# The output product of each expert block, written as three fp32r products with split operands

## The reference

```python
logits = xt @ router_w + router_b
scores = softmax(logits) + router_bias      # two groups of four, then the two best experts
def step(y, p):
    w1, b1, w2, b2, w3, b3, ge = p
    h = silu(xt @ w1 + b1) * (xt @ w2 + b2)
    return (y + ge[:, None] * (h @ w3 + b3), None)
y, _ = scan(step, zeros_like(xt), (ew1, eb1, ew2, eb2, ew3, eb3, gate.T))
z = silu(xt @ sw1 + sb1) * (xt @ sw2 + sb2) @ sw3 + sb3   # shared expert
x = x + y + z
```

## Time and profile before

| what | value |
|---|---|
| median of 3 runs | 371.08 us (370.57 to 374.64) |
| the profiled execution's own time | 369.3 us |
| its span | 367.5 us |
| TensorE busy | 337.1 us, 92% of the span |
| VectorE busy | 184.3 us, 50% |
| ScalarE busy | 117.5 us, 32% |
| GpSimd busy | 102.7 us, 28% |
| `bh` products, line 1503 | 62.4 us, 496 records |
| output products, line 1476 | 31.6 us, 62 records |

### The profile page before, as it was taken

The page is one execution under the profiler, slowest core; times in us unless marked ns, Lnnn a source line. Parts: engine busy times, 40 slices in busy tenths (PEclk is TensorE's granted clock), DMA queues, the critical chain, the costliest instruction groups (busy, mean ns, idle before and its releaser), DMA issues.

```text
span 367.5 us, 5442 instructions
## 1 busy us (share of the span) xinstructions
PE 337.1 (92%) x1923; PEld 248.0 (67%) x1923; DVE 184.3 (50%) x366; ACT 117.5 (32%) x203; POOL 102.7 (28%) x131
## 2 busy tenths in 40 slices
PE   8878898999999989999896599899998999999993
PEld 3356687459888778887765334458887877888872
DVE  2636893446848613364258617935420346542267
ACT  0655301013373214363102653572221334222110
POOL 2050000423666776774230000199600000000000
PEclk9998999559999999999999579999999999999997
DMA  6899910155767676999969986000000000110003
GB/s 209 278 340 404 383 45 0 29 192 193 220 194 238 208 243 186 320 361 395 398 248 339 333 307 223 0 3 0 0 2 0 0 3 0 64 52 0 1 2 114
DMA packets 32313, 59.94 MB, mean 163 GB/s; under 512 B 6680, under 2 KB 7548, under 8 KB 32286
## 3 DMA queue, kind: packets, MB, share of 16 engines
q1 hardware_dynamic: 25182, 48.89, 38.2%
q0 software_dynamic: 5056, 8.49, 6.9%
q10 hardware_dynamic: 2048, 2.21, 1.8%
HBM read 55.02 MB, written 12.40 MB: 183 GB/s over the span
## 4 chain that ended last, share of the span: by engine, by line
PE 69%; DVE 11%; DMA 7%; issue 7%; ACT 3%; POOL 3%; ACTq 0%; POOLq 0%; DVEq 0%; SPq 0%
PE bank L1503 13%; PE bank L408 10%; PE bank L410 10%; PE bank L409 10%; PE bank L1476 5%; PE bank L1487 4%; PE bank L1470 3%; PE bank L1569 3%; DMA xrow<-xstage 2%; DMA yg<-ytok 2%; PE bank L1325 2%; DMA xg<-xrow,tokx 1%; DVE acc L1200 1%; DVE upl L1220 1%; PE bank L1407 1%
## 5 line engine op out<-in xcount | busy, mean ns | idle before, releaser
L1503 PE MATMUL bank<-xt,ew 128*128 128x128 f32 x496 | 62.4, 280 | 2.0 <-issue 2.0
L1503 PEld LDWEIGHTS bank<-xt,ew 128*128 128x128 f32 x496 | 59.3, 196 | 4.3 <-issue 4.1
L595 POOL DMA_INDIRECT xg<-xrow,tokx x31 | 33.1, 1067 | 56.3 <-DVE dstx L1025 33.1
L602 POOL DMA_INDIRECT ytok<-yout,dstx x31 | 31.8, 1027 | 30.7 <-DVE yout L1136 21.5
L1284 DVE TENSOR_TENSOR sq<-rel 128x512 f32<-128x512 f32 x16 | 13.4, 837 | 43.3 <-ACT rel L846 43.3
L756 ACT ACTIVATE xt<-bank 128x512 f32<-128x512 f32 x31 | 18.5, 597 | 41.4 <-PE bank L1470 41.3
L1476 PE MATMUL bank<-ew,bhid 128*128 128x512 f32 x62 | 31.6, 595 | 0.0
L1470 PEld LDWEIGHTS bank<-ident,xg 128*128 128x128 f32 x124 | 15.8, 146 | 18.3 <-issue 14.2
L408 PE MATMUL bank<-dnh,sqh 128*128 128x512 f32 x64 | 25.2, 393 | 1.8 <-DVE sql L1292 1.6
L408 PE MATMUL bank<-ah,uph 128*128 128x512 f32 x64 | 25.1, 392 | 0.0
L410 PE MATMUL bank<-dnh,sql 128*128 128x512 f32 x64 | 24.9, 389 | 0.0
(11 more groups left out here) (299 smaller groups left out, 612.0 us busy)
## 6 DMA issues: line engine op xcount, KB each, us to landing
ew<-in_L_ffn_ew SPq DMA_DIRECT2D x51, 256.0 KB, 3.7
ew<-in_L_ffn_ew SPq DMA_DIRECT2D x21, 512.0 KB, 7.8
toep<-kpad SPq DMA_DIRECT2D x4, 1536.0 KB, 11.6
yg<-ytok SPq DMA_DIRECT2D x8, 512.0 KB, 4.6
acc<-in_x SPq DMA_DIRECT2D x4, 512.0 KB, 7.3
xrow<-xstage ACTq DMA_DIRECT2D x4, 512.0 KB, 7.5
upraw<-in_L_ffn_up_w SPq DMA_DIRECT2D x1, 2048.0 KB, 10.4
dnraw<-in_L_ffn_down_w SPq DMA_DIRECT2D x1, 2048.0 KB, 13.3
```

The source lines that it names most:

```text
L595: pool.indirect_dma_start(xg[:, n % XGS, :], None, xrow, bass.IndirectOffsetOnAxis(ap=tokx[:, n:n + 1].bitcast(U32), axis=0), bounds_check ...
L602: pool.indirect_dma_start(ytok, bass.IndirectOffsetOnAxis(ap=dstx[:, n:n + 1].bitcast(U32), axis=0), yout[:, n % YOS, :], None, bounds_che ...
L1503: mm = pe.matmul(bank[2 + n % 2][:, w * P:(w + 1) * P], ew[:, ring(n), col + k * P:col + (k + 1) * P], xt[:, n % 2, k, :], start=(k == 0), ...
```

## The change

Line numbers in this section are those of the kernel before. The output product of block n becomes three fp32r products by `split3`. Per block, ACT writes the rounded `w3h` from the block's `w3` in the ring (128 x 512) and the rounded `bhh` from `bhid` (128 x 128). DVE writes the remainder of `w3` in place into the ring (`ewl`, the same memory as `ew`, 128 x 512) and the remainder of `bhid` (`bhl`, 128 x 128). `w3h` has two buffers over the memory of `silu`, `bhh` and `bhl` have three each. Every block's copies and remainders stand at fixed places of the two lists.

```diff
     silu = at(exp_reg, "silu", [P, 2, HALF])
...
+    r = [silu_at]
+    w3h = at(r, "w3h", [P, 2, T], F32R)
+    r = [toep_at]
+    ewl = at(r, "ewl", [P, RING, WCOLS], F32R)
...
+    bhl = at([early[0] - BHS * P * 4], "bhl", [P, BHS, P], F32R)
...
+    bhh = at(small, "bhh", [P, BHS, P], F32R)
...
             act.activation(bsil[:, n % 2, :], bank[2 + n % 2][:, 0:P], ACT.Silu, bias=b1).then_inc(bsil_ok, 1)
+            act.wait_ge(*weights_in(n))
+            wait(act, by_done, n - 1)
+            act.activation(w3h[:, n % 2, :], ew[:, ring(n), W3], ACT.Copy).then_inc(w3h_ok, 1)
             if n + 2 < NB:
                 x_copy(n + 2)
+            act.wait_ge(bhid_ok, n + 1)
+            act.activation(bhh[:, n % BHS, :], bhid[:, n % BHS, :], ACT.Copy).then_inc(bhh_ok, 1)
...
             if n >= 2:
                 y_copy(n - 2)
+            dve.wait_ge(w3h_ok, n + 1)
+            tt(ewl[:, ring(n), W3], ew[:, ring(n), W3], f(w3h[:, n % 2, :]), ALU.subtract).then_inc(w3l_ok, 1)
+            dve.wait_ge(bhh_ok, n + 1)
+            tt(bhl[:, n % BHS, :], bhid[:, n % BHS, :], f(bhh[:, n % BHS, :]), ALU.subtract).then_inc(bhl_ok, 1)
...
         def block_y(n):
-            pe.wait_ge(bhid_ok, n + 1)
+            pe.wait_ge(bhl_ok, n + 1)
+            pe.wait_ge(w3l_ok, n + 1)
             wait(pe, yout_ok, n - 1)
-            pe.matmul(bank[6 + n % 2][:, :], bhid[:, n % BHS, :], ew[:, ring(n), W3], start=True, stop=True)\
-                .then_inc(by_done, 1)
+            split3(pe, bank[6 + n % 2][:, :], lambda k: (bhh[:, n % BHS, :], bhl[:, n % BHS, :]),
+                   lambda k: (w3h[:, n % 2, :], ewl[:, ring(n), W3]), 1).then_inc(by_done, 1)
```

More of the change, by code:

```diff
@@ L132, in adaln_ffn_program @@
     sw3raw = at(exp_reg, "sw3raw", [P, SH * T])
+    silu_at = exp_reg[0]
     silu = at(exp_reg, "silu", [P, 2, HALF])
@@ L345, in adaln_ffn_program @@
     warm_ok = sem("warm_ok")
+    w3h_ok, w3l_ok, bhh_ok, bhl_ok = (sem(s) for s in ("w3h_ok", "w3l_ok", "bhh_ok", "bhl_ok"))
     b3_done, b3_added = sem("b3_done"), sem("b3_added")
```

## The result

The changed kernel takes 379.32 us, the median of four runs (378.82 to 379.84); the kernel before took 370.98 in four runs beside them. The ratio is 1.0203, with a 95% interval of 1.0137 to 1.0268. It is slower by 8.3 us. I had forecast 374.2 us in a range of 370 to 378.5: the sign is right, the size is not, and the time lies above the range. The profiled execution took 379.51 us, its span is 377.8 (369.3 and 367.5 before).

What follows compares the result with a forecast made beforehand. TensorE (92% busy) was taken to bound only blocks to 8 and 15 to 21, POOL 8 to 17, the DMA queue from 21. 3.4 + 0.4 - 0.9 + 0.2 = +3.1 us on 371.08 gave 374.2 us, range 370 to 378.5.

Steps and rivals of the forecast that it cites:

- what one block costs: Expert stage, TensorE: three fp32r products take 0.68 us instead of 0.86, so a block takes 2.91 us instead of 3.09.
- the lag of DVE in blocks 2 to 5 and ACT's place in it, +3.4: DVE falls behind in blocks 2 to 5, ACT's sines and exponential wait, and POOL's chain from block 6 starts 3.4 us later.
- DVE's own two operations take 1.01 (96.01 to 97.02): DVE's existing work per block, 1.01 us, counted with 0.88 of remainders and 2.3 of convolution steps as 4.2 us a block.
- One addition ... I add 0.4 (0 to 2): POOL, blocks 8 to 17: remainders with two SBUF inputs slow some seven indirect DMAs and the small operations, +0.4 us.
- the second rival: DVE and POOL slow each other from block 8 on; POOL sets the pace, 4.8 us more, 379 us; chance 0.17, slower.
- the 383 us of the prediction: Time if every POOL gather and scatter pair lost both remainders, 0.88 us, in every block, by the skill's rule taken literally.
- the weights of block 28 land as much later as their queue began: Blocks 21 to 30: bytes and rate unchanged, so these weights shift with their queue and TensorE's faster pace becomes waiting.
- -0.9: Blocks 17 to 21: five blocks give back 0.18 us each before the first Toeplitz tile is let go, -0.9 us.
- the clock: Rival: TensorE's clock falls in the waits before blocks 8 and 10; two blocks cost 6 us, 380 us; chance 0.06.
- the tail: After block 30: the last output product waits for its new operations, mostly hidden by a 1.20 us scatter wait; +0.2 us.

Runs made afterwards that it cites:

- early splits only: Three fp32r products with their copies and remainders in blocks 0 to 13 only, later blocks as in the kernel before; 376.16 us, 1.0116 against the kernel before.
- late splits: Three fp32r products with their copies and remainders in blocks 14 to 30 only, earlier blocks as in the kernel before; 372.63 us, 1.0032 against the kernel before.
- splits from block 8: Three fp32r products with their copies and remainders from block 8 on, blocks 0 to 7 as in the kernel before; 374.57 us, 1.0096 against the kernel before.
- products only: Changed kernel with three products per block of operands rounded in blocks 0 and 1, other copies and all remainders dropped; 372.55 us, 1.0022 against the kernel before.
- operations only: Changed kernel keeping all four new operations per block, but with one float32 product of the two remainders; 376.06 us, 1.0110 against the kernel before.
- useless matmuls: Changed kernel plus filler matmuls into an unused bank: four before block 15's transposes, five before block 28's input products; 376.96 us, 1.0123 against the kernel before.

## Why the prediction was right in sign and wrong in size

**Right: what one block costs, and what ACT and DVE pay.** I had a block at 2.91 us; it is 2.93. The three products take 0.78 from the first to the next operation, not 0.68; half of the saving came from the place ahead of them, which I hadn't counted, and made up for it. From `w3h` to the next operation it is 0.52, from `bhh` 0.22, from `ewl` 0.60, from `bhl` 0.20 (differences of starts in the same timelines), against 0.53, 0.22, 0.61 and 0.27.

**Right in mechanism, 0.8 too large: the lag of DVE in blocks 2 to 5 and ACT's place in it, +3.4.** DVE has no idle time from block 2 to the `bhid` of block 6 but 0.44 us at two fills with zeros, and that `bhid` starts at 108.38 (forecast 106.5, with a start of the stage that is 2.8 us later in this profile). From there to `bsil` of block 8 it is 7.2 us, forecast 7.1. The scatter of block 6 is 2.6 us later, not 3.4: mis-sized by 0.8. The size was lost in "DVE's own two operations take 1.01 (96.01 to 97.02)": in this stretch of 1.01 us DVE idled for some 0.15, and where DVE doesn't idle the two take 0.86 (104.23 to 105.09). With 0.20 for `bhl`, not 0.27, the four blocks took 15.8 us (`bhid` of block 2 at 92.61, of block 6 at 108.38) and not 16.8. The waits of TensorE before blocks 8 and 10 came out at 0.99 and 1.86 (forecast 1 to 2 and 2); that before block 7 did not come.

**Wrong: "One addition ... I add 0.4 (0 to 2)".** This term measured +2.2, and 2.3 with the lag taken away. I had looked at the indirect DMAs, and their mean grew only from 1.05 to 1.12 us. The price fell on the 15 small operations that I had named in the same sentence and not priced: one of 0.22 us takes up to 0.76 beside a DVE operation with two SBUF inputs. The rule in the second rival, that "only an operation that starts under one is lengthened", held, but 15 short operations in a row start under many. The rival "DVE and POOL get in each other's way throughout" had the mechanism and the wrong place: it is not throughout, since the lateness was 4.8 us at gather 15 and 3.6 at block 27.
The Trainium skill (SBUF — State Buffer, "Who interferes with whom") says that a DVE instruction with two SBUF inputs contends with a GpSimd instruction that reads SBUF, and one with at most one doesn't. The small operations agree: 0.76 beside `ewl`, 0.22 at the same place when the remainder's input comes from PSUM. That the loser is blocked for the whole instruction agrees with them too: the one at 122.58 ends 0.09 us behind the `ewl` of 122.57 to 123.25. For the DMAs that GpSimd issues the same section of the Trainium skill infers that a `tensor_tensor` doesn't hold them up, so the 383 us of the prediction stretched the rule beyond that section. The trace lies between: single scatters that started under such operations took 1.42 to 1.78 us instead of 1.0, while the mean of all 62 grew by 0.07.

**Wrong: "the weights of block 28 land as much later as their queue began", with "the bytes to be moved and the rate are as before", and -0.9 kept.** The rate is as before, the bytes are not. From the issue of the first Toeplitz pair to the products of block 28 it took 20.2 us before (155.71 to 175.89) and 22.7 after (162.93 to 185.62). The DMA view of exactly that stretch, before and then after (queue, packets, MB, share of the 16 engines; q1 is SP's, q0 POOL's gathers and scatters):

```profile
DMA packets 3630, 7.61 MB, mean 377 GB/s; under 512 B 490, under 2 KB 490, under 8 KB 3627
...
q1 hardware_dynamic: 2733, 5.27, 71.8%
q0 software_dynamic: 894, 2.31, 30.9%
```

```profile
DMA packets 4125, 8.74 MB, mean 385 GB/s; under 512 B 556, under 2 KB 556, under 8 KB 4123
...
q1 hardware_dynamic: 3077, 5.90, 71.1%
q0 software_dynamic: 1046, 2.81, 32.3%
```

1.13 MB more, at 385 GB/s, is 2.9 us. With the rate nearly the same a longer stretch must hold more bytes, so this count says what was moved and not yet why. POOL's part of it is 0.50 MB or 1.3 us, and it goes with TensorE's pace: q0 moves 2.31 MB in this stretch before and 2.34 with early splits only, where the late blocks have the float32 product, and 2.77, 2.79 and 2.79 with late splits, splits from block 8 and products only, where they have three (operations only, at the old pace, lies between with 2.55). The stretch of the kernel with splits from block 8 is nearly as long as before (20.5 us), so there it isn't the length that makes the bytes. In the timelines one more gather falls into the stretch: that of block 26 starts 0.29 us behind the issue of the first pair, where it was 0.73 ahead of it, and the last scatter starts 18.30 us behind it, not 19.25. That these bytes hold up the weights is not shown: with splits from block 8 they are all there, and block 28 comes only 0.3 us later behind the issue. The other part, 0.63 MB of SP's (SyncE's) own queue, follows no such rule: it is 5.27 before, 5.90 in the changed kernel, 5.34 with early splits, 5.57 with late ones and 5.03 with splits from block 8. Whether it is a backlog from before the stretch or the second pair of tiles, which was issued 5.1 us ahead of block 28 here and 1.7 before, stays open. So block 28 is 4.4 us later because its queue began later (the mechanism forecast, with 2.9), and 2.5 more behind that; those 2.5 are the failed step, and only part of them, if any, goes with POOL's bytes. The 1.75 us that TensorE had won since block 16 (forecast 0.9) only made its wait longer.

**Wrong: the clock, put at nothing in the sum and at 0.06 as a rival.** The waits before blocks 8 and 10 (0.99 and 1.86 us) cost no clock in this profile of the changed kernel; that was luck, for in two others with the same early blocks (early splits, useless matmuls) the input products of block 10 took 3.04 and 3.28 us behind the same wait. It fell in the two longer waits, for which I had foreseen no price at all, since the wait of 1.35 us before block 28 had cost nothing. The input products behind them took 1.7 and 1.5 us more, together half of the rival's 6 us. With the fillers block 30 comes 2.4 to 3.1 us earlier.

**Right in size, by another way: the tail.** I had +0.2 (0 to 0.6), in the shade of a scatter. From block 30 to the first convolution product it is 29.6 us before and after. But the chain of waits of the changed kernel no longer goes through that scatter; it goes through the wait of the last product for `bhl` (1.01 us) and the products behind it:

```profile
196.52 0.30 DVE bhl L1164
...
196.86 0.50 PE bank L416
...
206.63 0.75 DVE acc L1217
```

So this wait now lies on the path, though the way through it is no longer than the old one was.

In short, the steps that failed: the "one addition" of 0.4, which measured 2.2; the way to block 28, which was to give back 0.9 us and lost 1.6 more from block 16 on (5.35 to 6.91); and the clock, put at nothing. The lag, 0.8 too large, hid part of them.

What I claim as shown by an edit that takes it away: the lag, the port cost and, in the profile, the clock loss. The bytes before block 28 are counted, their price is not shown. Of the +7.5 us, lag (2.6) and port (2.2) make 4.8; the rest, 2.7, is clock and queue less what TensorE won. The shares of clock and queue in it are read from one profile and are not separated by a ratio.

## What to carry to other kernels

A saving on the busiest engine is worth what the stages leave of it: test it alone, without its costs (here 1.0022, nothing measurable), before working out what the costs are. When an operation with two SBUF inputs is added on DVE, price the small GpSimd operations beside it one by one, not only the DMAs. Where an engine waits for a full queue, don't take the bytes ahead of it as given: a faster pace went with 0.5 MB more of another queue in the same stretch here, though what that cost stayed open. And measure positions from a place behind the start-up noise, here block 2.

## What the runs showed of the hardware that I had not expected

- A GpSimd operation on 128 x 16 takes 0.22 us alone and 0.60 to 0.76 beside a DVE operation with two SBUF inputs. An indirect scatter took 1.44 us beside such operations (`rre_k`, two of 64 x 512) instead of 1.03, and 1.76 where it started under one of 128 x 784.
- TensorE's granted clock was 0.50 (1.2 GHz) after a wait of 3.71 us, and the next 16 matmuls took 3.62 us instead of 1.95. After waits of 4.85 and 5.46 us they took 3.56 and 3.43. Between those and the harmless ones the lengths overlap: 3.36 and 3.39 us before block 28 cost nothing in two profiles (2.02), while 3.10 and 3.58 ahead of block 14 cost 1.3 and 1.4 in the same two. The same 1.86 us before block 10 cost nothing in the changed kernel (2.05) and 1.1 us with early splits (3.04), and 2.32 us ahead of block 14 cost 1.6 with the operations only (3.58). So the length of one wait doesn't tell whether the clock falls.
- Some profiles started the expert stage up to 3.3 us apart with the same instructions ahead of it, more than most effects looked for here; from there to block 2 they differed by up to 1.5 us more, and behind block 2 by 0.03 where the lists are the same.
